# Both dense products behind the first group, and the first source row ahead of the last group, in the last tile of a graph network

## The reference, cut

```python
# first network: two attention layers (4 heads of 192, then 2 heads of 96), then a dense layer
def gat_conv(x, src, dst, W, a_src, a_dst, bias, H, C, n):
    h = (x @ W).reshape(n, H, C)
    s_src = (h * a_src).sum(-1)
    s_dst = (h * a_dst).sum(-1)
    e = leaky_relu(s_src[src] + s_dst[dst], 0.2)
    ee = exp(e - segment_max(e, dst)[dst])
    alpha = ee / segment_sum(ee, dst)[dst]
    return segment_sum(alpha[:, :, None] * h[src], dst) + bias
out2 = gat_conv(gat_conv(layer_norm(x)))
x = _layernorm(x + concatenate([x, out2]) @ Wu + bu)
# second network: two graph convolutions with symmetric normalisation
x = _layernorm(x + gcn_conv(relu(gcn_conv(x, W1)), W2))
```

## Time and profile before

| | us |
|---|---|
| median of 3 runs | 792.03 (791.98 to 793.08) |
| the profiled execution | 792.36 |
| its span | 790.4 |
| TensorE matmul, busy | 751.0 (95%) |
| VectorE, busy | 564.5 (71%) |
| ScalarE, busy | 321.3 (41%) |
| GpSimd, busy | 28.4 (4%) |
| mean granted TensorE clock | 0.983 |

### The profile page before, as it was taken

The page is one execution under the profiler, slowest core; times in us unless marked ns, Lnnn a source line. Parts: engine busy times, 40 slices in busy tenths (PEclk is TensorE's granted clock), DMA queues, the critical chain, the costliest instruction groups (busy, mean ns, idle before and its releaser), DMA issues. The chain is left out here.

```text
span 790.4 us, 12012 instructions
## 1 busy us (share of the span) xinstructions
PE 751.0 (95%) x4363; PEld 654.8 (83%) x4363; DVE 564.5 (71%) x972; ACT 321.3 (41%) x638; POOL 28.4 (4%) x41
## 2 busy tenths in 40 slices
PE   6999999998999999999998987999999999999997
PEld 5967677775667889999766887898999999999996
DVE  4599988765999999999599997794743431413554
ACT  5456766764424334335154553562113331310000
POOL 7100000000000020000000020000000000000000
PEclk9999999998989999999999999899999999999999
DMA  9400000000000321100000500000000003000111
GB/s 308 173 2 1 1 2 1 2 1 1 1 0 1 104 98 68 42 27 1 0 1 25 193 1 15 27 2 0 1 1 1 1 1 121 0 1 1 73 68 57
DMA packets 10689, 28.17 MB, mean 36 GB/s; under 512 B 691, under 2 KB 4095, under 8 KB 10116
## 3 DMA queue, kind: packets, MB, share of 16 engines
q1 hardware_dynamic: 9940, 27.04, 9.7%
q10 hardware_dynamic: 688, 0.32, 0.1%
HBM read 23.48 MB, written 3.88 MB: 35 GB/s over the span
## 5 line engine op out<-in xcount | busy, mean ns | idle before, releaser
L1264 PE MATMUL ps<-g,att 128*128 128x193 f32 x800 | 133.3, 328 | 4.3 <-DVE att L724 2.9
L1264 PEld LDWEIGHTS ps<-g,att 128*128 128x128 f32 x800 | 130.3, 190 | 7.1 <-DVE att L724 2.9
L1096 ACT ACTIVATE att<-att,ssrc 128x1250 f32<-128x1250 f32 x60 | 80.2, 1338 | 99.6 <-DVE att L763 99.4
L763 DVE SCALAR_TENSOR_TENSOR att<-uB,s 128x1250 f32<-128x1250 f32 x60 | 90.6, 1514 | 0.0
L1264 PE MATMUL ps<-wp,xT 128*128 128x388 f32 x240 | 87.5, 502 | 2.6 <-ACT xT L979 2.6
L1264 PE MATMUL ps<-ctr,yhi 128*128 128x512 f32 x360 | 88.0, 352 | 0.0
L724 DVE SCALAR_TENSOR_TENSOR att<-att,ct 128x1250 f32<-128x1250 f32 x60 | 87.2, 1455 | 0.7 <-ACT att L1096 0.5
L865 DVE TENSOR_TENSOR ylo_a<-ps,yhi 128x512 fp32r<-128x512 f32 (+2 forms) x34 | 16.1, 528 | 77.3 <-ACT yhi L947 77.3
L1264 PE MATMUL ps<-ctr,ylo_a 128*128 128x512 f32 (+3 forms) x288 | 70.2, 352 | 0.1
L1264 PEld LDWEIGHTS ps<-ctr,yhi 128*128 128x128 f32 x360 | 64.1, 188 | 5.8
L1264 PEld LDWEIGHTS ps<-wp,xT 128*128 128x128 f32 x240 | 42.6, 190 | 26.0 <-issue 3.7
(11 more groups left out here) (244 smaller groups left out, 1331.4 us busy)
## 6 DMA issues: line engine op xcount, KB each, us to landing
uB<-u_dram SPq DMA_DIRECT2D x4, 1280.0 KB, 6.2
wux<-in_L_gnn_Wu SPq DMA_DIRECT2D x2, 2304.0 KB, 15.8
gw<-in_L_gnn_W SPq DMA_DIRECT2D x2, 2304.0 KB, 10.4
out<-ybuf SPq DMA_DIRECT2D x9, 384.0 KB, 2.3
xs<-in_x SPq DMA_DIRECT2D x1, 3072.0 KB
w<-in_L_gnn_W SPq DMA_DIRECT2D x2, 1152.0 KB, 8.0
w2x<-in_L_gnn_W SPq DMA_DIRECT2D x1, 576.0 KB, 10.5
wuo<-in_L_gnn_Wu SPq DMA_DIRECT2D x1, 576.0 KB
```

What stands on the lines that cost most here:

```text
L763: v.scalar_tensor_tensor(att[:, att_place(n), 0:N], uB[:, hp % 2, 1, 0:N], s08[:, h, q:q + 1], uB[:, hp % 2, 0, 0:N], ALU.add, ALU.max).th ...
L1096: a.activation(at_, at_, ACT.Exp, bias=ssrc[:, h, q:q + 1]).then_inc(att_exp, 1)
L1264: return t.matmul(o, lhsT, rhs, start=start, stop=stop, **kw)
```

## The change

In the last tile, TensorE does both dense products behind group 0 (before: one behind group 0, one behind group 1), ahead of tile 8's count transposes. ScalarE takes both out at the start of w = 1, behind `counts_out(8)`. VectorE makes the source scores ahead of both windows' one-hots of group 3 (before: between them). TensorE transposes the scores behind group 2 and spreads source row 0 ahead of group 3; ScalarE copies the three pieces ahead of group 3's window. The pieces 1 and 2 lie in banks 4 and 6, since bank 2 and 3 held dense products. The first maxima write one of their two scrap outputs elsewhere (`scrap0b`). After the tiles, tile 9's count transposes stand first on TensorE, and `counts_out(9)` ahead of `x_transposed(0)` on ScalarE.

```diff
+        scrap0b = at("scrap0b", [P, NP], BF16, R_BIG + 28672)
...
-            return (7, 2, 3)[n] if n < 3 else 4 + n % 4
+            return (7, 4, 6)[n] if n < 3 else 4 + n % 4
...
-                place = ((scrap1, scrap1b) if h < H1 else (scrap, scrap2b))[done % 2]
+                place = ((scrap1, scrap1b if h > 0 else scrap0b) if h < H1 else (scrap, scrap2b))[done % 2]
...
+                if gr == NG - 1:
+                    source_scores()
                 for s, unit in enumerate((unit_a, unit_b)):
...
-                    elif s == 0:
-                        source_scores()
...
-                    if last and 0 < w < 3:
-                        dense_out(q, w - 1)
+                    if last and w == 1:
+                        dense_out(q, 0)
+                        dense_out(q, 1)
...
                     if w == 2 and last:
                         row_copy(0, sRow1)
+                        for n in range(3):
+                            source_piece(n)
...
-            for n in range(3):
-                source_piece(n)
+            counts_out(T - 1)
             x_transposed(0)
-            counts_out(T - 1)
             counts_done(T - 1, 1)
...
-                    elif s == 0:
-                        t.wait_ge(vec_ready, 1)
-                        t.wait_ge(cp_deg, 3 * q + 4)
-                        t.transpose(ps[0:VR, 5, 0:P], svec[:, :].bitcast(F32), identf[:, :]).then_inc(row_ps, 1)
...
-                    if not last or w < 2:
-                        k = w if last else w // 2
+                    for k in ((0, 1) if w == 0 else ()) if last else (w // 2,):
...
+                    if w == 2 and last:
+                        t.wait_ge(vec_ready, 1)
+                        t.wait_ge(cp_deg, 3 * q + 4)
+                        t.transpose(ps[0:VR, 5, 0:P], svec[:, :].bitcast(F32), identf[:, :]).then_inc(row_ps, 1)
+                        t.wait_ge(row_out, 1)
+                        source_rows(0, 3)
...
-            t.wait_ge(row_out, 1)
+            t.wait_ge(bc_out, 3)
+            count_transposes(T - 1, 1)
             t.wait_ge(dn_out, 2 * T + 2)
-            source_rows(0, 3)
-            count_transposes(T - 1, 1)
-            t.wait_ge(bc_out, 3)
             x_transposes(0)
```

## The result

The changed kernel takes **794.36 us** (median of 20 runs, 792.24 to 797.79) against 792.09 of the kernel before, run beside it (20 runs, 790.52 to 793.25): 2.3 us more, a ratio of 1.003 (95% interval 1.0019 to 1.0041). It is slower, by 0.3%. Its span is 792.4 us (790.4).

What follows compares the result with a forecast made beforehand. VectorE's path was taken to bound this part, with a deadline on TensorE's x*Wu chain. Chain 2.5+1.5 = 4.0 late made VectorE 2.9 us late at tile 4: 792.0+2.9 = 794.9 us, range 792.4 to 796.8.

Steps and rivals of the forecast that it cites:

- ScalarE takes the gain of the earlier product: Last tile: `counts_out(8)` stands ahead of both `dense_out` in ScalarE's order, so VectorE's scores come 1.9 us later.
- The row comes earlier, VectorE only a little: Last tile: source rows start 2.5 us earlier on TensorE, but VectorE's maxima of head 0 start only 0.9 us earlier.
- Group 3 late, `counts_out(9)` in the chain: End of edge stage: late window copy and `counts_out(9)` ahead of `x_transposed(0)` make x*Wu of tile 0 2.2 to 2.7 late.
- Half clock in x*Wu: TensorE's x*Wu of tile 0 runs partly at half clock after pauses: 1.0 to 2.5 us lost, 1.5 taken.
- The deadline: Source 2, first head: VectorE needs tile 4's x*Wu product, slack 1.1 us; stops of 2.6 before head 1's maxima, 1.2 here.
- B: Rival: same late chain without half clock in x*Wu, 0.9 to 1.5 us slower, 793.2 us; chance 0.25.
- C: Rival: the early row wins, VectorE starts its maxima 0.9 us earlier and keeps that, 791.1 us; chance 0.12.
- E: Rival: later scores mean the row comes no earlier for VectorE; tile 4 still decides, 794.9 us; chance with forecast A 0.55.

Runs made afterwards that it cites:

- dense-only run: Kernel before with only the change's dense part: both products behind group 0, both `dense_out` at w = 1 behind `counts_out(8)`; 794.37 us against 791.91, ratio 1.0029.
- the run with TensorE kept busy: Changed kernel with 40 matmuls of no use in TensorE's waits; 792.94 us against 792.06 of the kernel before, ratio 1.0004.
- `x_transposed(0)` first: Changed kernel with ScalarE doing `x_transposed(0)` ahead of `counts_out(9)` again; 793.39 us, ratio 1.0018 to the kernel before.
- early row only: Changed kernel without its dense part: product 1 behind group 1 again, taken out at w = 2; 792.50 us against 791.91 before, ratio 0.9999.
- the version that beats both: Changed kernel without its dense part, and x tile 0's transposes and their copies ahead of group 3; 788.76 us against 791.91 before, ratio 0.9951.

## Why the prediction was right

Forecast was 794.9 (+2.9), measured 794.36 (+2.3); slower, by the mechanism named.

- **ScalarE takes the gain of the earlier product.** Scores forecast 1.9 later; 12.79 against 10.95 in d is 1.84. Shown alone by the dense-only run.
- **The row comes earlier, VectorE only a little.** Here a term was mis-sized: from the second pair of one-hots to the end of the last extra one I put 4.10 as before. It took 3.41 (185.02 to the end at 188.43): the idle 0.69 before the first extra one-hot, charged as part of the work, is gone (186.13 has no idle time before it). In the trace of before it reads

```profile
184.66 0.29 DVE L596 TENSOR_TENSOR xohs<-iota,sloT 128x256 bf16 x1 [0.69 <-issue]
```

  It is there again in the dense-only run (185.90) and absent in all six runs that, like the change, make the scores ahead of both windows, so it goes with the scores standing between the windows; why it does is not shown. The maxima began 1.7 early, not 0.9.
- **Group 3 late, `counts_out(9)` in the chain.** Forecast 2.2 to 2.7, measured 2.0: the upper end, which was for transposes at half clock as they ran, less the same 0.69. Each other term came as computed: one-hot to window copy 1.34 (1.31), transposes at half clock to mask 1.12 (1.1), `counts_out` 3.11 (3.10), copies to x*Wu 1.02 (1.01).
- **Half clock in x*Wu.** Forecast 1.5, in this trace 9.14 less 7.52 = 1.6; the run with TensorE kept busy gave 1.4 of the kernel's time back. That the clock would be low into x*Wu was my estimate: in the trace of before it was back at 193.1, ahead of x*Wu at 194.34. It is the weakest step in the grounds, since no row showed x*Wu behind such pauses, and the one that varies most: in the traces of the other orders with a pause ahead of it, x*Wu took 7.52 (`x_transposed(0)` first), 9.71 (dense only) and 10.53 (early row only). That the median of 20 runs came within 0.6 of the sum is in part luck, as the runs of one program spread over 5.5. By a pause alone the clock cannot be told: in the trace of after x*Wu starts at 0.50 behind an idle 1.60, but the clock had been at 0.50 since 185.2, ahead of that pause; in the same trace the transpose of the scores at 184.03 ran at full clock behind an idle 1.16, x*Wu did so behind 0.73 in the trace of before, and in the version that beats both the clock stayed full through pauses of 1.35 and 0.62.
- **The deadline.** Forecast stops of 2.6 and 1.2; 3.00 and 1.24. The chain is 3.60 late; less the slack of 1.12 (247.94 less 246.82) that is 2.48, and the memset stands 0.09 behind the product's end: 2.57 late. The sum stands 0.6 over the median; with the measured 3.6 in place of 4.0 it would give 794.5.
- **Rivals.** B (793.2) fits by its time the runs with clock 0.985 (792.8), of which no trace was taken, and the run with matmuls added (792.94), whose x*Wu ran at full clock. C fell in this order of work, but its gain exists: it appears as soon as the transposes of x tile 0 stand ahead of group 3. Above the range, which ends at 796.8, lie two of the 20 runs, 797.71 and 797.79, both with clock 0.975; no run at that clock was traced. E did not happen: the row did come earlier for VectorE. VectorE's second extra one-hot did not wait for the matmul of the first: the idle 1.11 before it has the same length where TensorE was still busy with other things (187.84 after, with the first extra matmul only at 188.10).

## What to carry to other kernels

Before work is moved ahead, look up who takes it out: an earlier matmul behind which the copying engine had 3.1 us of other work queued gave a later result (here by 1.84 us). Look also for the engine that has no idle time but a second input, and measure the slack of that one (here 1.1 us, at a wait that the profile before does not show, because it was met in time). And ask of a pause of TensorE two prices, the waiting and, in some runs, half clock in the long product behind it (here 9.14 us for x*Wu of tile 0, which took 7.52 at clock 1.00).

## What the runs showed of the hardware

Forty useless matmuls, 5.5 us of TensorE's time in their trace (1.25, 0.49, 0.71 and 3.07), made the kernel 1.4 us faster; in its trace x*Wu behind them ran at granted clock 1.00 (7.45 us) and not partly at 0.50 (9.14 us). And the fall of the clock does not stand at a fixed place of the program. The changed kernel and the one with `x_transposed(0)` ahead of `counts_out(9)` do the same work up to 191.4, with starts 0.14 apart; the clock fell at 185.2 in the one and at 190.5 in the other. Between 20 runs of one program the time differed by 5.5 us, for the most part in step with the mean clock (792.8, 794.6 and 797.7 at 0.985, 0.979 and 0.975), so a median of few runs of such a kernel can be off by as much as this change is worth.
